# A four-layer transformer block on one core: conversions, row sums and router products in another order

## The chip, the cores and the metric

The kernel runs on one core of a Trainium2 chip. The metric is the device time of one execution in microseconds (us), taken as the median of several executions. The core's engines work side by side, each through its own queue of instructions in order: TensorE (PE in the profile, PEld its weight loads), VectorE (DVE), ScalarE (ACT), GpSimd (POOL), and SyncE (SP), which issues DMA transfers. They meet at semaphores: an instruction at the head of a queue waits for a count, and everything behind it waits too.

## What is computed

Input `x` is 4 batches of 512 tokens of 512 values; `ctx` has the same shape. Four residual steps follow, each on a layer norm of `x`, scaled by a tanh gate:

```python
x = x + tanh(g_xattn[0]) * L0_xattn(layernorm(x), ctx)   # fp8-quantised product
x = x + tanh(g_ffn[0])   * L0_ffn(layernorm(x), w1, w2)  # two ternary products, gelu twice
x = x + tanh(g_xattn[1]) * L1_xattn(layernorm(x), ctx, ctx, mask, Wq, Wk, Wv, Wo)
x = x + tanh(g_ffn[1])   * L1_ffn(layernorm(x), router_w, gate_w, up_w, down_w, shared weights)
# L1_xattn, per batch and head h of 16 (4 key groups of 4 heads, 32 values each):
scores = Q @ K.T / sqrt(32) + slope[h] * (key - query);  w = softmax(masked scores);  out = (w @ V) @ Wo
# L1_ffn: logits = x @ router_w.T (8 experts); softmax; best two of eight; their gated MLPs,
# weighted; plus a shared gated MLP of width 704 with biases
```

## The kernel before, in words

The program is a row of blocks with a barrier between them. Three matter here.

**The ternary feed-forward** (up to about 299 us) walks 16 tiles `t` of 128 tokens. VectorE does, for each tile, `quantise_hidden(t-1)`, `add(t-2)`, the maximum of the hidden row, `columns_hidden(t-1)`, and then `ahead(t)` and `for_attention(t)`, which put in work for later stages. TensorE needs what `quantise_hidden` made before `turn_hidden`.

**Attention** (`stage_attention`, from 299 to 682 us). Every float32 operand of a large product is split into a float16 high part and a float16 low part, and a product is three matmuls (high by high, high by low, low by high). ScalarE makes a high part, VectorE then subtracts it from the value and so makes the low part. Work is laid out in 16 blocks (`BLOCKS`: 4 batches by 4 heads of a group) of 8 steps, 128 steps in all. In a step:

- TensorE makes two score tiles in key-by-query form (`p_pair`, called `p_col` in the code), which ScalarE turns into probabilities `prob` with an exponential; and two score tiles in query-by-key form (`p_row`, `row_scores`) for the block after, whose row maxima VectorE takes (`maxima`). `p_row` has two banks, so the first row tile of a step may start only when the first of the two maxima of the step before is done.
- In each second step TensorE multiplies probabilities by values (`values`).
- "Fills" (`FILLS`) are put between, in the bank pair `p_fill`: projections of keys (`k`), of queries (`q`), of values (`v`), results (`y`), sums of probabilities (`sum`) and the maxima turned into rows (`top`). A projection of keys or queries that TensorE ends in a step is read in the next step: ScalarE, after the two exponentials of that step, writes its high part into `halves` (`high(f)`), and VectorE its low part (`low(f)`), which waits for that high part (`t_high`). The list `late` holds such fills from one step to the next. There are 20 such projections, four of them ahead of the 128 steps; the other 16 are `late`: four queries of the batch's own last head, three keys, nine queries of a next batch.
- GpSimd adds the probability tiles of a block (`add_tiles`), so that TensorE need sum only the result and the fourth tile with a matrix of ones.

VectorE's code of a step before the change:

```python
for r in rows_at(blk, inb):
    maxima(*r)
...                      # norms, statistics, low parts of token rows
for f in late:
    low(f)
late = []
for f in fills_at(b, s):
    if f.kind in (*LATE, "top"):
        late.append(f)
    else:
        low(f)
```

After the last step, `last_sums` makes the row sums of the last block, `values` its last product, and `result` the output projection of the last batch, ahead of the barrier at 682 us.

**The shared expert and the router** (`stage_shared`, 682 to 829 us). TensorE makes six pairs of hidden chunks for batch 0, then the router's logits (`router`: 16 token tiles, 4 slices of 128, three passes), then `down(0)`. `low_rows` makes the low part of the last batch's normalised rows, which four DMA transposes (`turn(LATE_B)`) turn into columns that `router` needs. Routed expert tiles follow to the end.

Of the kernel before, what the change touches and what calls it, by code (L numbers as in the profile page):

```python
# [6 lines left out]
ALU = mybir.AluOpType  # L7
# [138 lines left out]
def stage_cross_ternary(nc, sb, ps, sem, st, place, a, x_d, ctx_d, x, gates, ident, identb, ones, neg_half, identq, keep, spare, early, x_slots):  # L146
# [95 lines left out]
    with nc.Block() as block:  # L242
# [432 lines left out]
        def _(dve):  # L675
# [197 lines left out]

            def for_attention(t):
                if t == 10:
                    first_statistics()
# [108 lines left out]
class Early:  # L985
# [4 lines left out]
    def __init__(self, nc, sb, sem, st, place, mstg, p_pair, a, ctx_d):  # L990
# [12 lines left out]
        self.t_ctx, self.t_w, self.t_mask, self.t_cols = (sem("t_" + n) for n in ("ctx", "w", "mask", "cols"))  # L1003
# [76 lines left out]
def stage_attention(nc, sb, ps, sem, st, a, early, ctx_d, x, gates, ident, identb, ones, neg_half, identq, keep, spare, bias, spent, rows_d,  # L1080
# [43 lines left out]
    stats = sb(st, "astats", [P, TPB, 6], F32)  # L1124
    mv = sb(st, "amv", [P, TPB, 2], F32)
    veps = sb(st, "aveps", [P, TPB], F32)
# [16 lines left out]
    names = ("zero", "const", "splith", "split", "veps", "rstd", "ln", "fill", "high", "free", "place0", "place1", "copy0", "copy1", "row", "max", "topl",  # L1143
             "topc", "tops", "col", "exp", "pv", "out", "sums", "acc", "lsum", "den", "spread", "inv", "invd", "rec", "scaled", "oh", "ol", "dve",
             "mcol", "any", "rows", "lo", "loh", "lol", "bz", "b", "kh", "rh", "rl", "part", "count")
    (t_zero, t_const, t_splith, t_split, t_veps, t_rstd, t_ln, t_fill, t_high, t_free, t_place0, t_place1, t_copy0, t_copy1, t_row, t_max, t_topl,
# [97 lines left out]
    with nc.Block() as block:  # L1244
        @block.sync
        def _(sp):
# [110 lines left out]
            for blk in range(BLOCKS):  # L1357
# [13 lines left out]
                if f:  # L1371
                    copy(f)
                    if j < HPG // 2:
                        place(f)
                if blk + 1 < BLOCKS:
                    place_top(blk + 1)
                if f and j >= HPG // 2:
                    place(f)
# [3 lines left out]
                if b == 0 and j in (0, HPG - 1):  # L1382
                    load_ctx(2 if j == 0 else 3)
                if blk == BLOCKS - 3:
                    lead_in()
# [11 lines left out]
        def _(pool):  # L1397
# [17 lines left out]
            def normalise(n):  # L1415
# [11 lines left out]
                if n == 0:  # L1427
                    pool.wait_ge(t_split, KB + 1)
# [27 lines left out]
            for blk in range(BLOCKS + 1):  # L1456
# [12 lines left out]
                if blk < BLOCKS:  # L1469
# [5 lines left out]
        def _(act):  # L1475
# [64 lines left out]
            def room(step):  # L1540

                old = step - PROBS
                if old >= 0:
# [3 lines left out]
                    if k < KB - 1:  # L1547
# [55 lines left out]
        def _(pe):  # L1603
# [17 lines left out]
            def fill_(f, part=None):  # L1621
# [23 lines left out]
                else:  # L1645
                    if f.n == 0:
                        pe.wait_ge(t_ol, HPG * f.batch + (HPG // 2 if part == 0 else HPG))
                        if f.batch == 0 and part != 1:
                            pe.wait_ge(t_split, 1 + KB)
# [55 lines left out]
            for b in range(B):  # L1705
                for s in range(STEPS):
# [17 lines left out]
                    if s + b and pr == 0:  # L1724
                        values(KB * blk + k - 1)
                    next_rows(4)
# [10 lines left out]
            last_sums()  # L1737
# [34 lines left out]
        def _(dve):  # L1772
# [75 lines left out]
            def last_inverse(half):  # L1848

                q = slice(half * S // 2, (half + 1) * S // 2)  # L1850
                dve.wait_ge(t_lsum, 1)
# [1265 lines left out]
```

## Time and profile before

| what | value |
|---|---|
| median of three runs | 1098.27 us |
| the profiled execution's own time | 1093.31 us |
| span of its instructions | 1091.5 us |
| TensorE busy over the span | 942.2 us (86%) |
| VectorE, ScalarE, GpSimd busy | 728.3, 581.4, 517.6 us |
| mean granted TensorE clock | 0.967 of 2.4 GHz |

The profile is one execution. Busy times of an engine say how much of the span it had work under way; ends of matmuls are modelled. The times below are counted from the start of the span. The profiled execution is 5 us faster than the median, and 1.8 us of it lie outside the span.

### The profile page before, as it was taken

The numbers are of one execution on the slowest core, as the hardware profiler recorded it, in microseconds if no ns is written. First come the engines' busy times: TensorE is split into PE (matmuls) and PEld (weight loads), VectorE is DVE, ScalarE is ACT, GpSimd is POOL, SyncE is SP. The second block draws the span as 40 slices with busy tenths as digits, with TensorE's granted clock in tenths as the row PEclk, the third lists the DMA queues.
The fourth block names the chain that finished last, engine by engine and source line by source line (L and its number), as shares of the span: only waits on it lengthen the run. The fifth ranks groups of instructions, "written<-read, shape, count | busy, mean of one in ns | idle before, by whom it ended". The sixth has DMA issues, their size and how long they took to land. (4 is left out here: it accounts for less than half of the span.)

```text
span 1091.5 us, 17844 instructions
## 1 busy us (share of the span) xinstructions
PE 942.2 (86%) x5602; PEld 436.3 (40%) x5620; DVE 728.3 (67%) x1416; ACT 581.4 (53%) x881; POOL 517.6 (47%) x547
## 2 busy tenths in 40 slices
PE   0466679999778999999998977979999999999995
PEld 0333345555332323333332312444445555556642
DVE  6988988888777787686677774768343534333247
ACT  5897989999536776766666670523131111111120
POOL 1100434553314576665675693103715888860065
PEclk9988899999998999999999998989999999999997
DMA  9322950000433543342412241895653988956588
GB/s 328 134 77 77 300 182 1 2 1 2 78 102 92 131 86 109 89 84 60 99 46 60 60 90 48 213 347 164 253 164 73 211 212 211 205 140 146 149 305 293
DMA packets 195588, 148.07 MB, mean 136 GB/s; under 512 B 133764, under 2 KB 162436, under 8 KB 195000
## 3 DMA queue, kind: packets, MB, share of 16 engines
q1 hardware_dynamic: 186568, 118.07, 40.1%
q0 software_dynamic: 8080, 27.60, 7.7%
q10 hardware_dynamic: 864, 1.44, 0.4%
q8 instruction: 41, 0.67, 0.2%
q14 instruction: 35, 0.29, 0.1%
HBM read 73.03 MB, written 44.02 MB: 107 GB/s over the span
## 5 line engine op out<-in xcount | busy, mean ns | idle before, releaser
L1840 DVE CUSTOM_DVE_ANT_0 ajunk<-p_row,mask_row 128x512 bf16<-128x512 f32 x256 | 166.2, 686 | 72.1 <-PE p_row L1666 65.2
L1577 ACT ACTIVATE prob<-p_pair,mask_col,any_key 128x512 f32<-128x512 f32 x168 | 121.7, 774 | 65.4 <-PE p_pair L1721 64.9
L1666 PE MATMUL p_row<-ks,early_place 99*128 99x512 f16 x256 | 98.9, 388 | 17.4 <-DVE top L1840 15.8
L1721 PE MATMUL p_pair<-early_place,ks 101*128 101x512 f16 x256 | 98.1, 387 | 7.1 <-ACT prob L1577 4.8
L1577 ACT ACTIVATE early_place<-p_pair,mask_col,any_key 128x512 f32<-128x512 f32 x88 | 63.8, 774 | 31.3 <-PE p_pair L1721 31.1
L2933 PE MATMUL s_down<-mw,shT 128*128 (+5 forms) x396 | 75.8, 379 | 3.7 <-DMA shT<-shidr 3.4
L3013 DVE SCALAR_TENSOR_TENSOR shid<-p_pair,ssilu 128x352 f32<-128x352 f32 x36 | 18.9, 524 | 89.6 <-PE p_pair L2918 89.5
L2847 ACT ACTIVATE ssilu<-s_gate 128x352 f32<-128x352 f32 x36 | 16.7, 463 | 109.4 <-PE s_gate L2918 109.4
L2835 POOL DMA_INDIRECT mw<-y_slots,dest x32 | 32.1, 1003 | 74.9 <-DMA y_slots<-spare 65.5
L2918 PE MATMUL s_gate<-mw,spare 128*128 (+1 forms) x504 | 66.6, 313 | 0.4 <-issue 0.4
L2918 PE MATMUL p_pair<-mw,spare 128*128 (+1 forms) x504 | 66.4, 313 | 0.0
L600 PE MATMUL po<-w2T,ctxT 128*128 128x512 bf16 x241 | 55.9, 379 | 2.8 <-ACT ctxT L491 2.0
L2302 POOL DMA_INDIRECT x_slots<-mw,dest x24 | 27.2, 1131 | 62.4 <-DVE dest L2629 55.4
L3015 DVE TENSOR_TENSOR shidr<-shid,shidr 128x352 f16<-128x352 f32 x36 | 41.3, 1148 | 22.7 <-ACT shidr L2851 22.7
L2851 ACT CAST shidr<-shid 128x352 f16<-128x352 f32 x36 | 17.5, 485 | 70.8 <-DVE shid L3013 65.4
L1453 POOL TENSOR_TENSOR early_place<-early_place,prob 128x512 f32<-128x512 f32 x36 | 50.2, 1428 | 5.5 <-ACT prob L1577 5.5
L1420 POOL TENSOR_TENSOR o<-raw_o,rec 128x512 f32<-128x512 f32 x15 | 19.9, 1328 | 68.9 <-DMA rec<-inv_d 68.9
L2918 PEld LDWEIGHTS s_gate<-mw,spare 128*128 128x128 f16 (+1 forms) x504 | 40.9, 102 | 25.5 <-issue 2.8
L1721 PEld LDWEIGHTS p_pair<-early_place,ks 101*128 101x128 f16 x256 | 24.8, 98 | 63.6 <-ACT prob L1577 22.0
L2918 PEld LDWEIGHTS p_pair<-mw,spare 128*128 128x128 f16 (+1 forms) x504 | 41.4, 102 | 19.5
L1666 PEld LDWEIGHTS p_row<-ks,early_place 99*128 99x128 f16 x256 | 24.8, 98 | 59.9 <-DVE top L1840 38.0
L298 POOL TENSOR_TENSOR rstd<-veps,neg_half 128x4 f32<-128x4 f32 x4 | 4.1, 1020 | 91.7 <-DVE veps L701 91.7
(453 smaller groups left out, 2287.1 us busy)
## 6 DMA issues: line engine op xcount, KB each, us to landing
x_slots<-nought SPq DMA_DIRECT2D x6, 1536.0 KB, 12.9
y_slots<-spare SPq DMA_DIRECT2D x36, 256.0 KB, 2.7
early_place<-in_ctx SPq DMA_DIRECT2D x8, 1024.0 KB, 5.7
early_place<-halves_d SPq DMA_DIRECT2D x45, 128.0 KB, 2.5
halves_d<-halves SPq DMA_DIRECT2D x18, 256.0 KB, 2.0
x<-in_x SPq DMA_DIRECT2D x4, 1024.0 KB, 7.4
w<-in_L_ffn_w SPq DMA_DIRECT2D x1, 4096.0 KB, 18.0
w<-in_L_ffn_w SPq DMA_DIRECT2D x4, 1024.0 KB, 4.8
```

What stands on the lines that cost most here:

```text
L600: mm = nc.tensor.matmul(py[:], q2T[t % 2][:, k, :], w2T[:, k, :], start=(k == 0), stop=(k == IB - 1))
L1420: nc.gpsimd.tensor_tensor(o[:], raw_o[n % 2][:], rec[:], ALU.mult).then_inc(t_scaled, 1)
L1453: nc.gpsimd.tensor_tensor(a[:, 2 * pr + c, :], prob_of(m, pr)[:, c, :] if k == 1 else a[:, 2 * pr + c, :], prob_of(m + k, pr)[:, c, :], AL ...
L1577: nc.scalar.activation(prob_of(KB * blk + k, pr)[:, c, :], p_col[c][:], ACT.Exp, bias=mask_col[:, b, k:k + 1], scale=any_key[:, b:b + 1]). ...
L1666: nc.tensor.matmul(p_row[n % 2][:], qs[0:ROWS_R, j, g, t * P:(t + 1) * P], ks[b % 2][0:ROWS_R, g, :], start=True, stop=True).then_inc(t_ro ...
L1721: nc.tensor.matmul(p_col[c][:], ks[b % 2][0:ROWS_C, g, k * P:(k + 1) * P], qs[0:ROWS_C, j, g, :], start=True, stop=True).then_inc(t_col, 1)
L1840: nc.vector.tensor_tensor_reduce(junk[:, n % 2, :], p_row[n % 2][:], mask_row[:, blk // HPG, :], 1.0, -3e38, ALU.add, ALU.max, top[blk % 2 ...
L2302: nc.gpsimd.indirect_dma_start(out=x_slots, out_offset=bass.IndirectOffsetOnAxis(ap=dest[:, s, t:t + 1], axis=0), in_=row_of(t), in_offset ...
L2835: nc.gpsimd.indirect_dma_start(out=gathered[:, t, s, :], out_offset=None, in_=y_slots, in_offset=bass.IndirectOffsetOnAxis(ap=dest[:, s, t ...
L2918: mm = nc.tensor.matmul(bank[n][p0:p1, 0:EI], (first_xT[:, n] if first(r) else xT[n])[:, hs, k, p0:p1], columns(e, c, EI), start=(k == 0 a ...
L2933: mm = nc.tensor.matmul(p_down[n][p0:p1, :], hT[n][0:rows(m), hs, m, p0:p1], columns(e, c, D, rows(m)), start=(m == 0 and hs + hm == 0), s ...
L3015: nc.vector.tensor_tensor(hidr[n][:, 1, 0:EI], hid[:], hidr[n][:, 0, 0:EI], ALU.subtract).then_inc(e_hl, 1)
```

## The change

It has six parts.

1. In `stage_attention`, VectorE takes the `late` low parts at the head of a step, ahead of the step's two maxima.
2. The statistics of batch 1's rows move out of the head of the attention loop into tile 9 of the feed-forward, and the low part of `W_o` (128x2048) becomes four pieces of 128x512 in steps 2 to 5.
3. For the last block, GpSimd adds nothing; TensorE sums each of the four probability tiles with ones, one after each `values`.
4. SyncE places the own last query after the maxima's rows, and issues four weight loads (`lead_in`) one block earlier.
5. The router's high and low weight parts lie side by side in one tile: a high token part meets both at once (16 columns), a low token part only the high weights (8 columns); the two halves of the logits are added where they were copied. The waits for the turned batches stand at each batch's first tile.
6. `low_rows` moves one chunk earlier.

The core of the diff:

```diff
+            def next_statistics():
+                dve.wait_ge(b_added, 2 * TPB)
+                for k in range(TPB):
+                    blink(nc.vector.bn_stats(early.stats[:, k, :], x[:, TPB + k, :]))
...
             def for_attention(t):
+                if t == 9:
+                    next_statistics()
...
-                if blk < BLOCKS:
+                if blk < BLOCKS - 1:
                     add_tiles(blk)
...
-            def last_sums():
-
-                pe.wait_ge(t_out, BLOCKS - 1)
-                pe.wait_ge(t_acc, ADDS * BLOCKS)
-                four(p_out[BLOCKS % 2], lambda g: ones[:, 0:DH], lambda pr, c: acc_of(BLOCKS - 1)[:, 2 * pr + c, :], True, False)
-                pe.wait_ge(t_exp, 4 * KB * BLOCKS)
-                four(p_out[BLOCKS % 2], lambda g: ones[:, 0:DH], lambda pr, c: prob_of(KB * BLOCKS - 1, pr)[:, c, :], False, True).then_inc(t_lsum, 1)
+            def last_sums(k):
+
+                m = KB * (BLOCKS - 1) + k
+                pe.wait_ge(t_exp, 4 * (m + 1))
+                if k == 0:
+                    pe.wait_ge(t_out, BLOCKS - 1)
+                four(p_out[BLOCKS % 2], lambda g: ones[:, 0:DH], lambda pr, c: prob_of(m, pr)[:, c, :], k == 0, k == KB - 1).then_inc(t_lsum, 1)
...
-            for t in range(TPB):
-                stat(1, t)
-            variances(1)
-            split_low(KB)
             dve.wait_ge(t_mcol, 2 * B)
...
+                    for f in late:
+                        low(f)
+                    late = []
                     for r in rows_at(blk, inb):
                         maxima(*r)
...
+                    if b == 0 and 2 <= s < 2 + KB:
+                        last_split_low(s - 2)
...
-                    for f in late:
-                        low(f)
-                    late = []
...
                     for k in range(KB):
-                        for hs, hm in passes:
-                            mm = nc.tensor.matmul(p_logit[:, t, :], xT[b][:, hs, k, c:c + P], rwT[hm][:, k, :],
-                                                  start=(k == 0 and hs + hm == 0), stop=(k == KB - 1 and hs == 1))
+                        for h in range(2):
+                            e = (2 - h) * EXPERTS
+                            mm = nc.tensor.matmul(p_logit[:, t, 0:e], xT[b][:, h, k, c:c + P], rwT[:, k, 0:e],
+                                                  start=(k + h == 0), stop=(k == KB - 1 and h == 1))
...
-            hidden(0, lambda: (low_part(2), statistics()), lambda: (low_part(3), normalise()), lambda: low_parts(4, 5),
-                   lambda: (low_rows(), ready_router(), low_parts(6, 7)), lambda: low_parts(8, 9), lambda: low_part(10))
+            hidden(0, lambda: (low_part(2), statistics()), lambda: (low_part(3), normalise()), lambda: (low_parts(4, 5), low_rows()),
+                   lambda: (ready_router(), low_parts(6, 7)), lambda: low_parts(8, 9), lambda: low_part(10))
```

The order of instructions, place one: VectorE in the eighth step of the first block, where the low part of a key projection (`halves1`, the second of two such buffers) is made. `ISA ajunk,top0` is a row maximum, the `ISA top0` behind it fetches its result. Before:

```order
362 L1840 ISA ajunk,top0<-p_row0,mask_row 128x512
363 L1840 ISA top0 128x1
364 L1840 ISA ajunk,top0<-p_row1,mask_row 128x512
365 L1840 ISA top0 128x1
366 L1886 TENSOR_TENSOR keep<-xn,keep 128x512 x2
367 L1803 SCALAR_TENSOR_TENSOR halves1<-p_fill0,halves1 128x512
368 L1840 ISA ajunk,top0<-p_row0,mask_row 128x512
```

The same place after:

```order
365 L1820 SCALAR_TENSOR_TENSOR halves1<-p_fill0,halves1 128x512
366 L1857 ISA ajunk,top0<-p_row0,mask_row 128x512
367 L1857 ISA top0 128x1
368 L1857 ISA ajunk,top0<-p_row1,mask_row 128x512
369 L1857 ISA top0 128x1
370 L1909 TENSOR_TENSOR keep<-xn,keep 128x512 x2
```

The low part moved from behind the two maxima and two subtractions to ahead of them; its wait for ScalarE moved with it.

Place two: TensorE at the end of the last block, where `p_out1` takes probabilities by values and `p_out0` the sums. Before:

```order
1089 L1721 MATMUL p_pair<-early_place,ks1 128x512 x4
1090 L1618 MATMUL p_out1<-prob4,v1_1 32x512 x2
1091 L1618 MATMUL p_out1<-prob5,v1_1 32x512 x2
1092 L1721 MATMUL p_pair<-early_place,ks1 128x512 x2
1093 L1618 MATMUL p_out0<-early_place,ones 32x512 x8
1094 L1618 MATMUL p_out1<-early_place,v1_1 32x512 x4
1095 L1733 MATMUL p_fill1<-wh,oT0 128x512
```

The same place after:

```order
1092 L1736 MATMUL p_pair<-early_place,ks1 128x512 x4
1093 L1633 MATMUL p_out1<-prob4,v1_1 32x512 x2
1094 L1633 MATMUL p_out1<-prob5,v1_1 32x512 x2
1095 L1633 MATMUL p_out0<-prob4,ones 32x512 x2
1096 L1633 MATMUL p_out0<-prob5,ones 32x512 x2
1097 L1736 MATMUL p_pair<-early_place,ks1 128x512 x2
1098 L1633 MATMUL p_out0<-early_place,ones 32x512 x4
1099 L1633 MATMUL p_out1<-early_place,v1_1 32x512 x4
1100 L1750 MATMUL p_fill1<-wh,oT0 128x512
```

Sums of four matmuls stand behind each product with values, and four fewer at the end, none of which reads what GpSimd added.

## Rows read from the trace of the kernel before

**Rows 1.** Windows, the attention loop: busy us of PE, PEld, DVE, ACT, POOL; clock; DMA

```profile
345.00:640.00 295.00, 282.67 (x1640) 94.53 (x1639) 213.76 (x599) 206.50 (x323) 193.41 (x162) 1.00 0.33 81
```

**Rows 2.** Groups by line, 345 to 640 us: busy, mean ns | idle before, releaser

```profile
L1666 PE MATMUL p_row<-ks,early_place 99*128 99x512 f16 x225 | 85.7, 381 | 6.2 <-DVE top L1840 6.0
...
L1803 DVE SCALAR_TENSOR_TENSOR halves<-p_fill,halves 128x512 f16<-128x512 f32 x16 | 11.0, 690 | 6.4 <-ACT halves L1491 6.3
```

**Rows 3.** Timeline around step 3 (own last query): start, us, engine, line, operation

```profile
345.64 0.38 PE L1666 MATMUL p_row<-ks,early_place 99*128 99x512 f16 x1
...
346.31 0.60 ACT L1491 ACTIVATE halves<-p_fill 128x512 f16<-128x512 f32 x1
...
347.56 0.68 DVE L1840 CUSTOM_DVE_ANT_0 ajunk<-p_row,mask_row 128x512 bf16<-128x512 f32 x1
...
348.30 0.39 PE L1666 MATMUL p_row<-ks,early_place 99*128 99x512 f16 x1 [0.28 <-DVE top L1840]
```

**Rows 4.** Timeline, high part and next step's first row tile: key, first and second query

```profile
355.46 0.59 ACT L1491 ACTIVATE halves<-p_fill 128x512 f16<-128x512 f32 x1
...
356.14 0.38 PE L1666 MATMUL p_row<-ks,early_place 99*128 99x512 f16 x1
...
376.11 0.38 PE L1666 MATMUL p_row<-ks,early_place 99*128 99x512 f16 x1
...
376.20 0.59 ACT L1491 ACTIVATE halves<-p_fill 128x512 f16<-128x512 f32 x1
...
385.92 0.59 ACT L1491 ACTIVATE halves<-p_fill 128x512 f16<-128x512 f32 x1
...
386.46 0.38 PE L1666 MATMUL p_row<-ks,early_place 99*128 99x512 f16 x1
```

**Rows 5.** Windows as in rows 1, two stretches at the lower clock

```profile
329.20:332.60 3.40, 3.23 (x9) 1.01 (x9) 3.21 (x9) 2.62 (x3) 0.00 (x0) 0.50 0.99 186
336.00:342.80 6.80, 5.25 (x16) 0.94 (x17) 6.12 (x17) 2.84 (x4) 2.90 (x3) 0.50 0.17 50
```

**Rows 6.** Timeline, the first steps of the attention loop

```profile
330.95 2.87 DVE L1776 BATCH_NORM_STATS2 astats<-x 128x6 f32<-128x512 f32 x4
...
337.30 0.61 PE L1666 MATMUL p_row<-ks,early_place 99*128 99x512 f16 x1 [3.49 <-DVE top L1840]
...
344.04 0.38 PE L1721 MATMUL p_pair<-early_place,ks 101*128 101x512 f16 x1
```

**Rows 7.** Timeline, feed-forward tile 9 to 10

```profile
242.65 1.28 DVE L811 TENSOR_SCALAR w<-w,b_k 128x2048 f32<-128x2048 f32 x1
...
245.59 0.61 PE L592 MATMUL po<-identq,w 128*128 128x128 f16 x8
```

**Rows 8.** Timeline, end of the last attention block

```profile
649.63 1.06 PE L1618 MATMUL p_out<-prob,v 128*32 128x512 f32 x8
...
651.34 1.45 ACT L1577 ACTIVATE early_place<-p_pair,mask_col,any_key 128x512 f32<-128x512 f32 x2 [0.75 <-PE p_pair L1721]
...
660.30 3.58 PE L1618 MATMUL p_out<-early_place,ones 128*32 128x512 f32 x16 [9.07 <-POOL early_place L1453]
...
664.67 0.39 PE L1733 MATMUL p_fill<-wh,oT 128*128 128x512 f16 x1
```

**Rows 9.** Timeline, low part of the last batch's rows, transposes, last hidden low part, router

```profile
702.30 0.75 DVE L2517 SCALAR_TENSOR_TENSOR mw<-p_pair,ebias,mw 128x512 f32<-128x512 f32 x1 [2.26 <-PE p_pair L2416]
...
705.88 5.30 SPq L2240 DMA_TRANSPOSE mw<-mw  x4
...
712.83 1.35 PE L2397 MATMUL p_pair<-rwT,spare 128*128 128x8 f16 x48 [2.79 <-DMA mw<-mw]
...
713.78 0.69 DVE L2535 SCALAR_TENSOR_TENSOR mw<-mw 64x512 f16<-64x512 f32 x1
...
719.86 1.53 PE L2397 MATMUL p_pair<-rwT,mw 128*128 128x8 f16 x52 [3.28 <-issue]
721.24 16.73 PE L2448 MATMUL p_down<-mw 128*128 128x512 f16 x68
```

More of the change, by code:

```diff
@@ L872, in rows_low @@
                 nc.vector.tensor_tensor(keep[:, c, D:2 * D], val_x[1][:, c, :], keep[:, c, 0:D], ALU.subtract).then_inc(b_xrows, 1)
+            def next_statistics():
+                dve.wait_ge(b_added, 2 * TPB)
+                for k in range(TPB):
+                    blink(nc.vector.bn_stats(early.stats[:, k, :], x[:, TPB + k, :]))
+                nc.vector.memset(pause[:], 0.0)
+                for k in range(TPB):
+                    ins = nc.vector.bn_aggr(early.mv[:, k, :], early.stats[:, k, :])
+                blink(ins)
+                nc.vector.tensor_scalar(early.veps[:], early.mv[:, :, 1], LN_EPS, None, ALU.add).then_inc(early.t_veps, 1)
             def for_attention(t):
+                if t == 9:
+                    next_statistics()
                 if t == 10:
@@ L1002, in __init__ @@
         self.cols = sb(st, "acols", [P, HEADS + 2], F32)
-        self.t_ctx, self.t_w, self.t_mask, self.t_cols = (sem("t_" + n) for n in ("ctx", "w", "mask", "cols"))
+        self.t_ctx, self.t_w, self.t_mask, self.t_cols, self.t_veps = (sem("t_" + n) for n in ("ctx", "w", "mask", "cols", "veps"))
+        self.stats = sb(st, "astats", [P, TPB, 6], F32)
+        self.mv = sb(st, "amv", [P, TPB, 2], F32)
+        self.veps = sb(st, "aveps", [P, TPB], F32)
     def raw(self, at, width):
@@ L1372, in _ @@
                     copy(f)
-                    if j < HPG // 2:
-                        place(f)
                 if blk + 1 < BLOCKS:
                     place_top(blk + 1)
-                if f and j >= HPG // 2:
+                if f:
                     place(f)
@@ L1725, in _ @@
                         values(KB * blk + k - 1)
+                    if blk == BLOCKS - 1 and k and pr == 0:
+                        last_sums(k - 1)
                     next_rows(4)
@@ L1735, in result @@
                 return mm
-            last_sums()
+            last_sums(KB - 1)
             values(KB * BLOCKS - 1)
@@ L1867, in split_low, with last_split_low @@
                 src, hi, lo = w_part(n)
+                nc.vector.tensor_tensor(lo, src, hi, ALU.subtract).then_inc(t_split, 1)
+            def last_split_low(q):
+                dve.wait_ge(t_splith, KB + 1)
+                src, hi, lo = (t[:, q * D:(q + 1) * D] for t in w_part(KB))
                 nc.vector.tensor_tensor(lo, src, hi, ALU.subtract).then_inc(t_split, 1)
@@ L2124, in stage_shared @@
     silu, hid = ([place(AT_SILU + (2 * i + n) * S * 4, S * 4, F32) for n in range(2)] for i in range(2))
-    rwT = [sb(st, f"rwT{n}", [P, KB, EXPERTS], F16) for n in range(2)]
+    rwT = sb(st, "rwT", [P, KB, 2 * EXPERTS], F16)
     logit = sb(st, "logit", [P, NT, EXPERTS], F32)
@@ L2363, in router_high @@
                 act.wait_ge(m_rwt, 1)
-                nc.scalar.copy(rwT[0][:], p_rw).then_inc(m_rwh, 1)
+                nc.scalar.copy(rwT[:, :, 0:EXPERTS], p_rw).then_inc(m_rwh, 1)
             high_parts(0, 1)
@@ L2390, in router @@
                 pe.wait_ge(m_rwl, 1)
-                for b in range(1, B):
-                    pe.wait_ge(m_xT[b], TURNED)
                 for t in range(NT):
                     b, c = t // TPB, t % TPB * P
+                    if b and c == 0:
+                        pe.wait_ge(m_xT[b], TURNED)
                     for k in range(KB):
-                        for hs, hm in passes:
-                            mm = nc.tensor.matmul(p_logit[:, t, :], xT[b][:, hs, k, c:c + P], rwT[hm][:, k, :],
-                                                  start=(k == 0 and hs + hm == 0), stop=(k == KB - 1 and hs == 1))
+                        for h in range(2):
+                            e = (2 - h) * EXPERTS
+                            mm = nc.tensor.matmul(p_logit[:, t, 0:e], xT[b][:, h, k, c:c + P], rwT[:, k, 0:e],
+                                                  start=(k + h == 0), stop=(k == KB - 1 and h == 1))
                 mm.then_inc(m_logit, 1)
```

28 lines of the change are left out of this document (15 added, 13 removed).

## The prediction

> **What bounds the kernel now.** I read the windows first, to see which engine fills each stretch. In the attention loop TensorE is busy 282.67 of 295 us at the full clock [rows 1], VectorE 213.76, ScalarE 206.50. So TensorE's queue sets the pace, and a pause in it is lost unless it takes the place of another pause. The groups by line then say how little it pauses: its row tiles wait 6.0 us in all for maxima [rows 2]. VectorE's 16 late low parts wait 6.3 us for ScalarE's high parts [rows 2], and that costs TensorE next to nothing, since the maxima that it needs have already been taken. The timelines show four places outside this rule: the first steps of the loop, where TensorE stands 3.49 us for VectorE [rows 6], the end of the last block, where it stands 9.07 us for GpSimd's additions [rows 8], the router, where it stands 2.79 us for the transposes and 3.28 us for nothing that the profile names [rows 9], and the head of each stage.
>
> **Part 1, low parts ahead of the maxima.** Here the wait for ScalarE goes in front of work that TensorE needs. In step 3 ScalarE's high part ends at 346.91 (346.31 + 0.60), VectorE's low part follows, the next maximum starts at 347.56, and the row tile that it frees starts at 348.30, which is 1.39 us after the high part's end [rows 3]. Before the change that tile is the first of step 5. After it the maximum is that of step 3 itself, so the tile freed is the first of step 4, which now starts at 345.64 [rows 3]. ScalarE's high part cannot come sooner, because it stands behind that step's exponentials. TensorE is held for 348.30 - 345.64 = 2.66 us, and queued behind the row tile are its second score tile, `values` and the fills; ScalarE's next exponential waits for that score tile.
>
> The same sum for the other kinds, high end + 1.39 less the next first row tile [rows 4]:
> - keys (3 times): 356.05 + 1.39 - 356.14 = 1.30;
> - first query of a next batch (3 times): 376.79 + 1.39 - 376.11 = 2.07;
> - second and third query (6 times, taken alike): 386.51 + 1.39 - 386.46 = 1.44;
> - own last query (4 times): 2.66.
>
> Together 3.90 + 6.21 + 8.64 + 10.64 = 29.4 us. Some of it replaces waits that are there: of the 6.0 us of waiting for maxima [rows 2] I let half fall into it, so I take **+26.5**. Bounds: +18, if all 6.0 us and as much again of ScalarE's and VectorE's backlog are absorbed; +32, if the second row tile of each step lags 0.2 us more. The low parts of `top` wait for a copy that ScalarE makes a step earlier, so they hold nothing; the maxima's rows land up to 1.3 us sooner, worth 1 us together with SyncE's new order (0 to 2).
>
> **The clock** is a cost that hangs on part 1. After a stretch of TensorE half idle the granted clock fell to 0.50 (1.2 GHz) for 3.4 us, and after the 3.49 us of waiting that ended at 337.30 it stood there from 336.0 to 342.8 [rows 5, 6]; through the whole loop, with only short waits, it stayed 1.00 [rows 1]. The new pauses of 2.07 and 2.66 us, seven of them, lie between the two cases. A fall of 3.4 us loses 1.7 us of work, one of 6.8 us with 5.25 busy loses 2.6 [rows 5]. I take three falls at 1.7, **+5**; bounds 0 and 7 x 2.6 = 18.
>
> **Part 2, statistics.** At the loop's head VectorE's statistics (2.87 us) and what follows go [rows 6]. TensorE then isn't stopped at 337.30 - 3.49 = 333.8 but goes on at ScalarE's pace: what is left there of two pairs of exponentials (1.45 a pair, half a pair gone: about 2.0 with the waits between), a product of 1.06 [rows 8] and six matmuls of some 0.22 (the 16.73 / 68 = 0.246 of [rows 9] are partly at the lower clock) make 4.4 us, so the score tile of step 3, now at 344.04 [rows 6], comes at about 338.2, **-5.8**; at least -2.5, if the clock falls all the same. The four pieces of `W_o` are each no longer than a low part (0.69 [rows 2]) and lie in steps in which VectorE waits for rows. In the feed-forward the same statistics (2.87 + about 0.65 of small operations) stand ahead of `quantise_hidden(9)`: it starts at 242.65 + 3.5 = 246.2 and ends at 247.4, while TensorE wants it at 245.59 [rows 7]: **+1.9** (0 to +3.5). GpSimd, `add(8)` and the next maximum are queued behind; VectorE waits later in each tile and catches up.
>
> **Part 3, the last block.** TensorE gets three sums of 1.06 us [rows 8] ahead of the last exponentials. ScalarE waits there for scores, so they push its last pair by about 2.6 us (0 to 3.2), from an end at 652.79 to 655.4 [rows 8]. The last sum and product take 2 x 1.06, and the first result starts at 657.6, not 664.67 [rows 8]: **-7.1** (-5 to -9). What is late next is not VectorE's reciprocal (it has 10 us until its half is needed, behind 36 results and `lead_chunk`), nor GpSimd, whose additions were the releaser [rows 8] and are gone.
>
> **Parts 5 and 6, router.** `low_rows` takes 2.28 us and goes into the 2.26 us in which VectorE waited at 702.30 [rows 9]. It ends by then, up to 3.5 us ahead of the transposes' start at 705.88 [rows 9]. I count 3, since SyncE may still be at the batch before. The router's start moves from 712.83 to about 709.9, when TensorE ends its chunks (712.83 - 2.79 = 710.0): that wait goes. 192 router matmuls become 128. The trace has them at 1.35 us for 48, some 27 ns each [rows 9]; with 16 columns one costs between that and twice that. I take it as unchanged, as 8 columns are far from filling 27 ns, which makes 3.4 us (up to 5.1). `down(0)` needs the last hidden low part, which ends at 713.78 + 0.69 = 714.5, so the end of the router is hidden from there on; it starts at 721.24 now [rows 9]. If the unexplained 3.28 us stay, it starts near 716.7, else at 714.5: -4.5 to -6.7, and the half clock of this stretch may lift for 1 us more. I take **-5.5** (-3 to -7.5).
>
> The Trainium skill, in "TensorE: Matmul & The Clock Gate", section "Wait — 56ns, not 53.3ns?", says that starts of matmuls come no closer than about 25 ns however few columns they have. By that the 16-column form costs what the 8-column form does and the router would take about 3.4 us, by twice the columns 5.1 us; no row here shows 16 columns.
>
> **The sum.** +26.5 + 5 - 5.8 + 1.9 - 7.1 - 5.5 - 1.0 = **+14**. The profiled execution at 1093.31 becomes about 1107; the median lies 5 us above it before, and I put the same distance on: 1098.27 + 14 = **1112 us**. Its own range is 1100 to 1121.
>
> **Rivals.**
> - *The low parts cost nothing* (0.18). If VectorE's queue stood with slack at these points, a stall would not reach TensorE. For it: VectorE is idle 295 - 213.76 = 81 us of the loop [rows 1]. Against it: the two row banks leave one step of slack, and 345.64 against 348.30 is more than a step's wait. The rest of the sum stays: -17.5, **1081 us**.
> - *The clock falls with each long pause* (0.17). Seven falls at 2.6 us, not three at 1.7, add 13: **1125 us**, more than 2% slower. It decides from the point at which a pause of 2.1 to 2.7 us acts like the one of 3.49 us and unlike the short waits of the loop, 6.0 us in all, after which no fall shows [rows 1, 2].
> - *The router keeps its time* (0.10): transposes land late behind the loads, the unnamed pause stays and moves: +5.5, **1118 us**.
>
> The Trainium skill's same page, section "HAM oscillation — how this bites in real kernels", tells of a kernel that waits before every burst of matmuls and pays the clock's fall in each round, which speaks against adding 16 pauses and for the second rival. By it the time is that rival's 1125; the trace shows falls after two long pauses only.
>
> **Chances.** The forecast has 0.55. Faster than 1076 us needs the first rival and gains at their bounds: 0.04. Above 1120 lies most of the second rival and the upper edge of the forecast and the third: 0.22. Within 2%, about what a measurement can tell from no change: 0.74. The range takes in the first rival's time: 1080 to 1127.
>
> **What the profile after would show.** Part 1: `halves` low parts at the head of steps, each behind an idle time "<-ACT halves", 20 us or more in all, and row tiles waiting for "DVE top" some 25 to 35 us in place of 6.0; the loop about 26 us longer. If those waits stay near 6, the first rival is right. Clock: 0.50 in stretches of the loop. Part 2: no wait of 3 us near 334, and one of about 2 us before the transposes near 246. Part 3: no idle of 9 us; results begin about 5 us after the last exponential. Parts 5 and 6: router right behind the chunks, `down(0)` 4 to 7 us sooner relative to the stage's start. I would be most wrong if ScalarE reaches its high parts sooner than today, since all of part 1 rests on when they end.

## The result, and the profile after

| | before | after |
|---|---|---|
| median of its runs | 1100.03 us (4) | 1126.69 us (4) |
| ratio, 95% interval | | 1.0252 (1.0206 to 1.0298) |
| profiled execution, its own time | 1093.31 us | 1122.37 us |
| its span, mean granted clock | 1091.5 us, 0.967 | 1120.6 us, 0.951 |

The change makes the kernel slower, by 26.7 us between the medians and 29.1 us between the two profiled executions. I forecast +14. The medians take in every execution, also one of 3382.5 us of the kernel before (the median of its other three is 1098.27 us) and, further down, one of 1154.75 us of part1_alone; the ratios leave both out.

I read the trace by landmarks, since both kernels issue the same TensorE work in nearly the same order. Times are starts of instructions: "step n" is the first score tile of step n, counted through all four batches.

| stretch, us | before | after | difference |
|---|---|---|---|
| start to the second group of transpositions of the feed-forward | 175.3 | 180.2 | +4.9 |
| from there to the last group | 117.4 | 119.3 | +1.9 |
| to step 0 | 37.2 | 40.0 | +2.8 |
| step 0 to 3 | 14.1 | 8.4 | -5.7 |
| step 3 to 111 | 272.6 | 312.8 | +40.1 |
| step 111 to the first result | 48.0 | 39.1 | -8.9 |
| to the shared expert's first chunk | 19.7 | 19.7 | 0 |
| to `down(0)` | 36.9 | 30.5 | -6.4 |
| to the end | 370.2 | 370.6 | +0.4 |

The first stretch lies ahead of every edit; over all fourteen kernels profiled here it took 175.3 to 180.3 us, and the execution of before stands at the lower end. Of the others, four behave as meant or as feared (tile 9, the loop's head, the last block, the router); one holds the result, the loop from step 3. Its windows in both kernels, of before and then of after:

```profile
core 0: us, PE busy (x) PEld busy (x) DVE busy (x) ACT busy (x) POOL busy (x), PEclk, DMA share, GB/s
344.00:616.70 272.70, 261.79 (x1526) 88.09 (x1524) 197.81 (x561) 189.09 (x295) 177.85 (x150) 1.00 0.32 80
```

```profile
348.00:660.70 312.70, 277.29 (x1525) 88.50 (x1523) 207.00 (x565) 192.63 (x295) 182.07 (x151) 0.95 0.30 74
352.77:356.18 3.41, 3.41 (x13) 0.73 (x13) 3.23 (x9) 1.62 (x4) 2.23 (x2) 0.50 0.11 42
400.56:407.38 6.82, 6.06 (x18) 1.20 (x19) 5.42 (x17) 3.50 (x6) 2.49 (x2) 0.50 0.28 74
```

As many matmuls (1526 and 1525 in the windows) take 15.5 us more of busy time, and TensorE stands idle for 35.4 us instead of 10.9. A pause makes the idle time; a lower clock makes the busy time longer. The second and third row of after are two of the eight stretches at clock 0.50 between step 3 and step 111 (seven of 3.4 us, one of 6.8); before had none there.

The groups by line of the same stretch of after, to be read beside [rows 2]:

```profile
L1681 PE MATMUL p_row<-ks,early_place 99*128 99x512 f16 x216 | 85.7, 397 | 33.8 <-DVE top L1857 33.7
L1820 DVE SCALAR_TENSOR_TENSOR halves<-p_fill,halves 128x512 f16<-128x512 f32 x16 | 11.1, 692 | 48.1 <-ACT halves L1504 48.1
```

VectorE waits 48.1 us ahead of its sixteen low parts, always for ScalarE, and TensorE's row tiles wait 33.7 us for maxima. Step 3, from the timeline of after, against [rows 3]:

```profile
349.23 0.39 PE L1736 MATMUL p_pair<-early_place,ks 101*128 101x512 f16 x1 [0.22 <-ACT prob L1592]
350.24 0.60 ACT L1504 ACTIVATE halves<-p_fill 128x512 f16<-128x512 f32 x1
350.88 0.69 DVE L1820 SCALAR_TENSOR_TENSOR halves<-p_fill,halves 128x512 f16<-128x512 f32 x1 [2.48 <-ACT halves L1504]
351.49 0.68 DVE L1857 CUSTOM_DVE_ANT_0 ajunk<-p_row,mask_row 128x512 bf16<-128x512 f32 x1
352.32 0.38 PE L1681 MATMUL p_row<-ks,early_place 99*128 99x512 f16 x1 [2.71 <-DVE top L1857]
352.97 0.78 ACT L1592 ACTIVATE prob<-p_pair,mask_col,any_key 128x512 f32<-128x512 f32 x1 [1.46 <-PE p_pair L1736]
```

The chain is high part, low part, maximum, row tile; the row tile starts 1.48 us after the high part's end at 350.84. Behind it, ScalarE then waits 1.46 us for the score tile queued behind the row tile. Right after this pause, at 352.77, the clock falls.

The other places, all TensorE's timeline of after: feed-forward tile 9 [rows 7], the head of the attention stage, the end of the last block [rows 8], and the router [rows 9]:

```profile
252.35 0.45 PE L592 MATMUL po<-identq,w 128*128 128x128 f16 x5 [1.67 <-DVE w L811]
...
327.60 0.39 PE L1681 MATMUL p_row<-ks,early_place 99*128 99x512 f16 x1 [2.66 <-DVE top L1857]
...
697.98 1.06 PE L1633 MATMUL p_out<-early_place,ones 128*32 128x512 f32 x8 [1.32 <-ACT early_place L1592]
698.87 1.04 PE L1633 MATMUL p_out<-early_place,v 128*32 128x512 f32 x8
699.84 0.39 PE L1750 MATMUL p_fill<-wh,oT 128*128 128x512 f16 x1
...
746.07 0.95 PE L2419 MATMUL p_pair<-rwT,spare 128*128 128x16 f16 x32
746.88 2.54 PE L2419 MATMUL p_pair<-rwT,mw 128*128 128x16 f16 x96
750.01 1.25 PE L2470 MATMUL p_down<-mw 128*128 128x512 f16 x5 [0.59 <-DVE mw L2495]
```

The second line is a wait at the head of the attention stage, behind which the clock stood at 0.50 from 328.9 to 342.5. In before, the wait at this place took 1.26 us, and in eleven of the twelve kernels below 1.7 to 2.2 us; 2.2 was in router_alone, which has before's code there. The 9.07 us wait for GpSimd is 1.32 us for ScalarE. The router's 128 matmuls run without a wait in 3.35 us, right behind the chunks. In this view a merged line names the form of its first matmul: half of the 128 have 16 columns and half 8.

### The profile page after: what moved, and what is told of

The parts are those of the page before. It is cut to its first block and busy times, and to the rows that moved or that the text cites. A ratio compares the mean times of both kernels' runs of the same rounds, so it can differ in the third digit from the quotient of the medians.

```text
span 1120.6 us, 17748 instructions
## 1 busy us (share of the span) xinstructions
PE 966.5 (86%) x5571; PEld 440.0 (39%) x5572; DVE 727.9 (65%) x1419; ACT 585.3 (52%) x881; POOL 501.4 (45%) x539
## 3 DMA queue, kind: packets, MB, share of 16 engines
q1 hardware_dynamic: 186568, 118.07, 40.2%
q10 hardware_dynamic: 864, 1.44, 0.4%
## 5 line engine op out<-in xcount | busy, mean ns | idle before, releaser
L1681 PE MATMUL p_row<-ks,early_place 99*128 99x512 f16 x256 | 103.7, 407 | 41.3 <-DVE top L1857 40.3
L2873 ACT CAST shidr<-shid 128x352 f16<-128x352 f32 x36 | 17.5, 485 | 69.0 <-DVE shid L3035 69.0
L3037 DVE TENSOR_TENSOR shidr<-shid,shidr 128x352 f16<-128x352 f32 x36 | 39.2, 1089 | 21.1 <-ACT shidr L2873 21.1
L1633 PE MATMUL p_out<-prob,v 128*32 128x512 f32 x336 | 49.1, 659 | 0.0
L2841 POOL TENSOR_TENSOR mw<-mstg,mw 128x1408 f16<-128x1408 f32 (+2 forms) x20 | 46.1, 2307 | 3.5 <-POOL mstg L2837 3.5
```

Of the source, the lines that this page charges most:

```text
L1633: mm = nc.tensor.matmul(bank_[g * DH:(g + 1) * DH, :], lhs(g), rhs(pr, c), start=start, stop=stop)
L1681: nc.tensor.matmul(p_row[n % 2][:], qs[0:ROWS_R, j, g, t * P:(t + 1) * P], ks[b % 2][0:ROWS_R, g, :], start=True, stop=True).then_inc(t_ro ...
L2841: nc.gpsimd.tensor_tensor(half(e, 1, q), s, half(e, 0, q), ALU.subtract).then_inc(m_wl, 1)
L3037: nc.vector.tensor_tensor(hidr[n][:, 1, 0:EI], hid[:], hidr[n][:, 0, 0:EI], ALU.subtract).then_inc(e_hl, 1)
```

## Experiments

All twelve ran beside the kernel before. The ratio is to the kernel before, with its interval; stretches, in us, are of each kernel's one profiled execution, and "falls in it" counts the stretches at clock 0.50 that begin between step 3 and step 111.

| kernel | median us | ratio (95%) | to step 0 | 0 to 3 | 3 to 111 | falls in it | 111 to result | to `down(0)` |
|---|---|---|---|---|---|---|---|---|
| lows_back | 1085.61 | 0.985 (0.977 to 0.994) | 40.3 | 9.5 | 278.5 | 1 | 39.2 | 29.5 |
| part1_alone | 1140.33 | 1.036 (1.026 to 1.045) | 38.5 | 14.0 | 317.3 | 10 | 47.1 | 37.3 |
| long_only | 1103.89 | 1.005 (1.002 to 1.008) | 43.3 | 8.4 | 295.4 | 5 | 39.1 | 30.6 |
| short_only | 1098.47 | 1.000 (0.996 to 1.004) | 37.0 | 8.2 | 290.1 | 2 | 39.1 | 29.6 |
| high_first | 1079.45 | 0.979 (0.973 to 0.985) | 40.3 | 9.5 | 274.1 | 0 | 39.1 | 29.6 |
| stats_alone | 1095.13 | 0.994 (0.990 to 0.997) | 40.5 | 9.6 | 274.7 | 1 | 47.0 | 36.9 |
| sums_alone | 1088.78 | 0.989 (0.982 to 0.995) | 38.5 | 14.0 | 272.7 | 0 | 39.2 | 34.5 |
| router_alone | 1088.65 | 0.986 (0.980 to 0.991) | 40.2 | 14.7 | 274.4 | 1 | 47.0 | 29.3 |
| keep_busy | 1112.01 | 1.014 (1.010 to 1.018) | 40.3 | 9.5 | 299.8 | 0 | 39.1 | 30.8 |
| high_first_spread | 1082.0 | 0.986 (0.982 to 0.991) | 39.5 | 9.3 | 274.3 | 0 | 39.1 | 29.6 |
| lows_back_places | 1079.06 | 0.984 (0.980 to 0.987) | 39.5 | 9.5 | 273.4 | 0 | 39.1 | 30.3 |
| high_first_lows_back | 1077.4 | 0.985 (0.981 to 0.989) | 38.7 | 9.5 | 275.8 | 1 | 39.1 | 29.2 |

### lows_back: the change without part 1

```diff
-                    for f in late:        # head of the step
-                        low(f)
-                    late = []
                     for r in rows_at(blk, inb):
                         maxima(*r)
 ...
+                    for f in late:        # end of the step, as before
+                        low(f)
+                    late = []
```

> The changed kernel with part 1 undone: the late low parts stand again behind the maxima of their step; all other parts stay. Theory (pauses and the clock falls that follow them): the changed kernel's steps 3 to 111 took 40.1 us longer than before, and all of it goes, the row tiles' waits for maxima fall from 41.3 us to under 8, and no stretch at clock 0.50 is left between step 3 and the last block. The profiled execution comes to 1122.4 - 40 = 1082, 1.3 to 2% below the kernel before. Rival (the other parts cost in the loop, W_o's pieces, the sums or SyncE's new order): over 10 us of the 40 stay, and the time is above 1092.

34.2 of the 40.1 us went. The waits of the row tiles for maxima fell to 4.8 us. What stayed, 5.9 us, has one place, step 14 (TensorE's timeline of this kernel):

```profile
377.93 1.01 PE L1625 MATMUL p_fill<-x_columns,wh 128*128 128x512 f16 x2 [4.34 <-DMA x_columns<-keep]
378.73 0.63 PE L1625 MATMUL p_fill<-x_columns,wl 128*128 128x512 f16 x1
```

The fill waits 4.34 us for transposes and then runs at half clock (0.63 us for one matmul). These transposes stand in SyncE's queue behind `place_top` and `place`, whose order the change had turned round.

### part1_alone: the kernel before with part 1

```diff
+                    for f in late:
+                        low(f)
+                    late = []
                     for r in rows_at(blk, inb):
                         maxima(*r)
```

(and the same three lines taken away at the step's end)

> The kernel before with part 1 alone: the low parts ahead of the maxima. Theory: +38 to +42 us, of which 27.6 are pauses of TensorE and 12.5 the eight clock falls, so about 1133 for a profiled execution and 3.5% above the kernel before. Rival (the falls came from the head of the loop, which the other parts changed): pauses alone, +28, 1121.

39 us by the ratio (3.55% of 1100; its interval runs from 28 to 50 us), 44.7 us between steps 3 and 111, with ten falls. Part 1 alone explains the loss. The pauses-only rival at +28 is out by the trace, not by the timing: the ten falls are there with the loop's head of before. The stretch is over the 42 expected by about what the two falls beyond those of the changed kernel cost (1.6 us each, see keep_busy).

### long_only and short_only: which pauses bring the clock down

```diff
+                    for f in late:
+                        if s in (3, 16) or f.kind == "top":       # short_only: if s not in (3, 16)
+                            low(f)
+                    late = [f for f in late if not (s in (3, 16) or f.kind == "top")]
                     for r in rows_at(blk, inb):
                         maxima(*r)
```

(the others are taken behind the maxima)

> The changed kernel with only the seven long-paused low parts ahead of the maxima (own last query in step 3 of a batch, first query of the next batch in step 16); keys' and the second and third queries' low parts go back behind the maxima. Pauses: 4 x 2.05 + 3 x 2.2 = 14.8 us. Theory A (falls follow the long pauses alone, as the forecast had it): nearly as many falls as in the changed kernel, 7 or 8, so 12 us more, 1082 + 27 = 1109. Theory B (every pause counts, short ones too): fewer falls than eight, three or four, 1082 + 15 + 6 = 1103.

> The changed kernel with only the nine short-paused low parts ahead of the maxima (keys in step 7, second and third query in steps 20 and 28 of a batch); the seven long ones go back behind. Pauses: 3 x 1.5 + 6 x 1.22 = 11.8 us. Theory A (falls follow the long pauses alone): no fall in the loop, 1082 + 12 = 1094. Theory B (every pause counts): falls in the loop, three or more at 1.6 us each, 1099 or more.

Steps 3 to 111 took 22.8 us more than before with the seven long pauses and 17.5 us more with the nine short ones. Neither theory on the clock held: theory A wanted no fall with the short pauses alone, where two came; theory B wanted three or more there, and with the long ones alone three or four, where five came. The falls follow pauses of both kinds, but not each one:

| pause | length | falls behind it, changed kernel | in long_only or short_only | in part1_alone |
|---|---|---|---|---|
| own last query | 2.7 us | 3 of 4 | 4 of 4 | 4 of 4 |
| first query of the next batch | 1.4 to 1.9 | 2 of 3 | 1 of 3 | 3 of 3 |
| second and third query | 1.28 | 3 of 6 | 2 of 6 | 3 of 6 |
| keys | 1.15 | 0 of 3 | 0 of 3 | 0 of 3 |

Two of these falls began up to 1.1 us ahead of the end of the pause, the others up to 2.4 us behind it. So longer pauses brought falls more often. The kernel before had such a pause too, in step 106, and its clock stayed at 1.00 behind it (TensorE's timeline of before):

```profile
605.08 0.39 PE L1666 MATMUL p_row<-ks,early_place 99*128 99x512 f16 x1 [1.50 <-DVE top L1840]
```

Eleven of the fourteen profiled kernels have this wait, of 1.45 to 1.72 us. In nine of them no fall follows; in stats_alone and router_alone it is the one fall of the stretch, 1.0 and 1.1 us behind the wait's end. One trace without a fall does not say that a pause of that length is free.

### keep_busy: the same pauses, filled

```diff
+                        if c == 0 and again:          # 10, 4, 8, 5, 5 times by the kind of pause
+                            need(pe, t_exp, 2 * (STEPS * b + s))
+                            for _ in range(again):
+                                nc.tensor.matmul(p_col[1][:], ..., start=True, stop=True)
                         next_rows(1)
```

> The changed kernel with its sixteen pauses left where they are, but filled: ahead of the row tile that waits, TensorE multiplies the step's second score tile 4 to 10 times into its bank for nothing (10 times after the own last query, 4 after keys, 8 and 5 and 5 after the next queries), before the real one. Theory (the eight falls to clock 0.50 in the loop come from these pauses, and cost 12.5 of its 40.1 us): no fall, or one, from step 3 on; steps 3 to 111 take 272.6 + 27.6 + about 2 for multiplications that outlast a pause, 302 us, instead of 312.8, though TensorE does more work; about 1110 for a profiled execution. Rival (the falls come for another reason, or cost nothing that the pauses would not cost anyway): falls stay, 312 us or more, 1122 or more.

VectorE's wait for high parts is as long as in the changed kernel (47.7 us against 48.1), so the pauses are all there, but the clock stays up:

```profile
348.80:648.70 299.90, 287.09 (x1632) 96.76 (x1631) 201.37 (x567) 191.98 (x295) 182.04 (x151) 1.00 0.29 77
```

With 106 useless matmuls more, steps 3 to 111 take 299.8 us, not 312.8. So of the 40.1 us 27.2 are pauses (299.8 - 272.6) and 13.0 clock. Useless matmuls that outlast a pause are counted with the pauses here; the windows of the changed kernel put it at 24.5 us more of idle and 15.5 us more of busy time, so the clock cost 13.0 to 15.5 us. The Trainium skill, "TensorE: Matmul & The Clock Gate", section "HAM oscillation — how this bites in real kernels", tells of a kernel that waits 3 to 5 us for a DMA behind each burst of matmuls and starts each next burst at the lower clock. The trace agrees that pauses bring the clock down, at 13.0 us for sixteen pauses, but these were shorter, 1.15 to 2.7 us, and only half of them were followed by a fall.

### high_first: ScalarE's high parts ahead of its exponentials

```diff
+                    for f in late:
+                        high(f)
+                    late = []
                     for c in range(2):
                         ...                       # the step's exponentials
-                    for f in late:                # behind them
-                        high(f)
-                    late = []
```

> The changed kernel with one more edit: ScalarE makes the late high parts at the head of a step, ahead of that step's exponentials instead of behind them. Theory (the pauses are TensorE waiting for maxima that wait for a low part that waits for ScalarE's high part behind its exponentials): VectorE's wait for high parts nearly goes, since each comes 1.45 us and more earlier, TensorE's waits for maxima fall from 41.3 us to 10 or less, and the sixteen high parts of 0.6 us each now delay exponentials, 0 to 0.6 us each, 5 us in all, so steps 3 to 111 take about 272.6 + 8 = 281 us instead of 312.8, with no or one clock fall, and the profiled execution comes to about 1090. Rival (the place of the low part costs by itself, through VectorE's queue): waits for maxima stay above 20 us, time above 1105.

The low parts stay ahead of the maxima. The high part of step 3 starts 0.49 us ahead of the exponentials and the row tile waits 0.36 us:

```profile
344.79 0.60 ACT L1504 ACTIVATE halves<-p_fill 128x512 f16<-128x512 f32 x1 [1.31 <-PE p_fill L1625]
...
345.42 0.69 DVE L1820 SCALAR_TENSOR_TENSOR halves<-p_fill,halves 128x512 f16<-128x512 f32 x1 [0.50 <-ACT halves L1504]
346.02 0.68 DVE L1857 CUSTOM_DVE_ANT_0 ajunk<-p_row,mask_row 128x512 bf16<-128x512 f32 x1
...
346.86 0.38 PE L1681 MATMUL p_row<-ks,early_place 99*128 99x512 f16 x1 [0.36 <-DVE top L1857]
```

Waits for maxima are 8.2 us (10 expected), steps 3 to 111 take 274.1 us (281 expected), no clock fall. So a low part ahead of the maxima costs next to nothing by itself; it costs while ScalarE's high part, for which it waits, stands behind the exponentials. VectorE still waits 19.7 us for high parts, which I had expected to nearly go, but TensorE doesn't wait with it. The delay of the exponentials, which I had put at 5 us, costs almost nothing: the whole stretch is 1.4 us longer than before. This version is 2.1% faster than the kernel before (1.5 to 2.7%).

### Parts alone: statistics, last sums, router

Each is the kernel before with the hunks of one part (5 and 6 together). Part 4 was not run alone.

> The kernel before with part 2 alone: the second batch's statistics in feed-forward tile 9 and W_o's low part in four pieces. Theory: TensorE waits about 1.7 us in tile 9 (the stage's tiles 1 to 15 take 119.3 instead of 117.4 us); at the loop's head the wait of 3.49 us goes, steps 0 to 3 take 8.4 us instead of 14.1; together -3.8, 1089.5 for a profiled execution, within 0.5% of the kernel before. Rival (moving the statistics also brings a later stall and a clock fall at the head of the attention stage, which the changed kernel's trace had): the stretch from the end of the feed-forward to step 0 takes 2 us or more longer than the 37.2 us of before, and nothing is gained.

Tile 9 cost 1.8 us and the head of the loop gave 4.5. The stretch up to step 0 was 3.3 us longer than before, as the rival said; but this stretch took 40.2 us in router_alone as well, which has before's code there, and 37.0 in short_only, which has the change's. It varies by 3 us and more from execution to execution, for instance with how long ScalarE takes to issue its twelve DMAs (8.10 us before, 8.82 after); over all runs it is 37.2 to 40.2 in four kernels without the moved statistics and 37.0 to 43.3 in ten with them. Whether the moved statistics add to it is left open. I had expected 1089.5 us for the profiled execution, and it took 1097.44; the ten timings are 0.6% faster than before (0.3 to 1.0%).

> The kernel before with part 3 alone: the last block's sums on TensorE. Theory: steps 111 to 127 take 1.5 us longer, the 9.07 us in which TensorE waited for GpSimd go, the last score tile to the first result takes 3.8 us instead of 14.0, together about -8.8 and the half-clock stretch of 10 us at this place goes too (its cost is in the 14.0); 1084.5 for a profiled execution. Rival (the time comes back later, since VectorE's and SyncE's work behind the last block gets late): the first result to the shared expert's first chunk takes more than the 19.7 us of before.

-8.8 us from step 111 to the first result, and the 19.7 us to the first chunk did not change: all is kept. The stretch up to `down(0)` was 2.4 us shorter as well, which I had not expected: the router, with its code of before, ran its 192 matmuls in one go in 5.1 us, without the unnamed pause of 3.28 us [rows 9].

> The kernel before with parts 5 and 6 alone: the router's two weight parts side by side in one matmul of 16 columns, and low_rows one piece earlier. Theory: from the shared expert's first chunk to the first down matmul 30.5 us instead of 36.9, -6.4, with the router's 128 matmuls at some 27 ns each like the 8-column ones; all of it kept to the end, 1087 for a profiled execution. Rival (given back in the expert stage, where the scatter and the loads set the pace): the stretch from down(0) to the end grows from 370.2 by as much.

-7.5 us up to `down(0)`, of which 3.3 are the unnamed pause. Since that pause is gone in sums_alone too, under the old router, that the router's edit removes it isn't shown. In this profiled execution the experts took 9.9 us longer, most of it in the two waits below and the 6.8 us at half clock behind the first; the timing over five runs is 1.4% faster, so it is this execution's and not a giving back:

```profile
942.23 3.70 PE L2919 MATMUL s_gate<-mw,spare 128*128 x12 [4.17 <-DMA spare<-x_slots]
951.87 1.96 PE L2919 MATMUL s_gate<-mw,spare 128*128 x12 [1.21 <-DMA spare<-x_slots]
```

### Versions that keep the gains

> ScalarE's high parts first (as in the run of that name) and the second batch's statistics not all in feed-forward tile 9 but spread: two in tile 9, one each in tiles 11 and 12, the variances in tile 13. Expected: TensorE's wait of 1.7 us in tile 9 goes, tiles 1 to 15 take 117.5 us instead of 119.3, nothing else changes; 1.8 us below that run, 1075.5 for a profiled execution. Rival (the pieces delay tiles 11 to 13, which have 1.4, 1.3 and 0.9 us of slack, and one is overdrawn): 119 us or more.

The feed-forward stretch came back to 117.2 us, as expected. The profiled execution did not show it, since its experts took 376.0 us instead of 370.3 (TensorE waited 4.3 us there for DMAs into `shT`, 0.5 in high_first), and by the timings it cannot be told from high_first.

> The changed kernel with part 1 undone, SyncE's order of before (a block's own last query is placed ahead of the maxima's rows in a batch's first blocks) and the statistics spread. Expected: the wait of 4.34 us for x_columns and the half clock behind it, which the run with the low parts back had at step 14, go, so steps 3 to 111 take 273 to 274.5 us instead of 278.5; with 1.8 us of the statistics 1081 for a profiled execution at 1089.1 + 1.8 before. Rival (W_o's pieces, not SyncE's order, brought that wait): 278 us stay.

```diff
                 if f:
                     copy(f)
+                    if j < HPG // 2:
+                        place(f)
                 if blk + 1 < BLOCKS:
                     place_top(blk + 1)
-                if f:
+                if f and j >= HPG // 2:
                     place(f)
```

The wait for `x_columns` fell from 4.34 to 0.3 us, and steps 3 to 111 took 273.4 us. So SyncE's order, not W_o's pieces, had brought it.

> ScalarE's high parts first, VectorE's low parts behind the maxima as before, statistics spread. Expected, if the place of the low part is free once the high part comes early: the same within 3 us as high_first_spread (274 us for steps 3 to 111, waits for maxima 8 us or less). If the low parts ahead of the maxima cost even then (VectorE waited 19.7 us for high parts in high_first), this one is 2 us or more better; if they are of use (rows placed sooner), it is 3 us or more worse.

Waits for maxima fell to 3.0 us, the best of all, but with SyncE's new order the wait for `x_columns` was back at 4.0 us, with a half-clock stretch behind it, and ate the gain (275.8 us). The new order in SyncE's queue needs the low part ahead of the maxima; with it behind, it costs. High parts first, low parts behind and SyncE's old order together were not run.

The intervals of these three and of high_first overlap: 1.4 to 2.1% faster than before, and which is best stays open.

## Why the prediction was right and wrong

- **What failed: the term "The clock".** "I take three falls at 1.7, +5; bounds 0 and 7 x 2.6 = 18." It measured +13.0 or more (changed kernel against keep_busy). The price of a fall was about right, 13.0 over eight falls is 1.6 us each. The count was wrong, eight and not three: five of the seven long pauses brought a fall, and three of the nine short ones, which I had let bring none, all of 1.28 us. I had reasoned from the loop's short waits of before, after which no fall shows. Most of them are fractions of a microsecond, and the one of 1.50 us, which the sum of 6.0 us hid, was followed by a fall in two other kernels.
- **The pauses.** +26.5 forecast, 24.5 to 27.2 measured. By kind they were 2.7, 1.4 to 1.9, 1.28 and 1.15 us, where I had 2.66, 2.07, 1.44 and 1.30; the sixteen together took 27.15 us, not 29.4. The 3 us that I let fall into waits that were there did not: all waits for maxima rose by 27.7 us. That 26.5 came so near is in part two misses that cancel. High part's end to row tile took 1.48 us in step 3 where I used 1.39. The way of reading it, the high part's end in the trace of before plus the chain behind it, set against the next row tile, held.
- **The rival "The clock falls with each long pause"** had more of the mechanism, and 1125 stands against a median of 1126.69. Its point of decision did not hold: with long pauses alone, five of seven brought a fall. Its 7 x 2.6 is 18 us, five above the 13.0 measured; the price of 2.6 was that of a fall of 6.8 us, and only one of the eight was that long. That its time comes so near is luck: these five make up for most of what is unassigned below.
- **"The low parts cost nothing"** is refuted by lows_back and part1_alone; **"The router keeps its time"** by the router's stretch.
- **Part 2.** Loop head -5.8 forecast, -5.7 measured (-4.5 to -5.9 in the other kernels with the moved statistics); tile 9 +1.9 forecast, +1.9 measured.
- **Part 3.** -7.1 forecast, -8.9 measured, inside its bounds. The first result starts 3.8 us after step 127's first score tile, and nothing behind it was late.
- **Parts 5 and 6.** -5.5 forecast, -6.4 measured. The unnamed pause in the router's second half is gone, as it is in sums_alone with the old router, so 3.3 of the 6.4 us are not shown to be these parts' work. The starts of the 128 matmuls lie 25 ns apart on average behind 16 columns and behind 8, as the rule of the Trainium skill that I cited has it; the 192 of before, all of 8 columns, started 26 ns apart.
- **SyncE's new order** I put at a gain inside the 1 us with "maxima's rows". In the changed kernel no cost of it shows; without part 1 it cost 4 us and more. I had taken the two edits as separate.
- **The rest.** 4.9 us of the 29.1 lie ahead of every edit and 2.8 us in a stretch that varies by as much between executions. The one execution profiled before was 6.7 us under that kernel's median here, and its mean granted clock of 0.967 is at the top of what that kernel had: in the 39 executions beside the experiments it was 0.949 to 0.967, with 0.956 in the middle. By medians the miss is 26.7 against 14: the clock is 8 of these 13 us, the larger gains take 3 off, and I cannot assign the rest, about 7 us, to an edit. The timings of the parts alone don't help: they add to +0.4% where the whole change is +2.5%, while their stretches (+44.7, -2.7, -8.8, -7.5) add to +25.7 us. In what stretches the other executions of the kernel before lose time, no trace shows.

The range (1080 to 1127) held the median by 0.3 us; the direction was right.

## What to carry to other kernels

When an operation is moved ahead of others, look at what it waits for on the other engine, and where that stands in that engine's queue: move both ends of the pair, or neither. Here one block moved on ScalarE turned +2.5% into -2.1%. And price a pause of the engine that sets the pace with the clock that it may take along: in this loop some 27 us of pauses brought at least 13 us of slower work, and pauses of 1.3 us were enough for some of it.

## What the runs showed of the hardware

- Whether the clock falls after a pause is not decided by the pause's length alone: with pauses of 2.7 us it fell 11 times in 12, with 1.4 to 1.9 us 6 in 9, with 1.28 us 8 in 18, with 1.15 us never in 9 (changed kernel, long_only, short_only and part1_alone together), and with the wait of 1.45 to 1.72 us in step 106 2 times in 11 kernels.
- Useless matmuls into a bank that is written again anyway kept the granted clock at 1.00 through sixteen such pauses, and the kernel was faster for it: 1112.01 us against 1126.69, each in its own comparison (ratios 1.014 and 1.025).
- The router's starts lie 25 ns apart whether a matmul has 16 columns or 8 (64 of each in the changed kernel), so a second set of 8 weight columns beside the first cost no time that shows.
- The same program's executions differ by up to 1.6% here (the kernel before took 1091.94 to 1109.36 us in 39 runs; one more, of 3382.5 us, stands far outside), with waits for single DMAs in the expert stage of 4 us and more; a part worth 5 us is read from its stretch of the trace, not from one total.
